# Decoder on one core: a slot table for the linear attentions, first keys and queries in the score banks, a zero block for the first bucket, the first norm's write behind the second norm's sums

## What is computed

```python
# first block: linear attention, causal by buckets of 64 tokens, 16 heads of 8 channels
q, k, v = split(x @ W_qkv.T)
q = softmax(q, axis=-1) * HEAD_DIM ** (-0.5)
k = exp(k)
# a bucket sees the sums of k and of k v over the buckets ahead of it; the first sees none
attn = q * context(shifted) / max(q . k_cumsum(shifted), 1e-06)
x = layernorm(x + attn @ W_out.T)
# second block: softmax attention a1 (16 heads of 32), then a2 on the context, each with its own
# norms and a gelu network; then a mixture of experts, a causal attention, a cross attention,
# a second mixture of experts, each with a residual and a layernorm
y = ln(x, ln1_g, ln1_b)
y = y + mha_a1(y, y);  y = ln(y, ln2_g, ln2_b);  x = layernorm(x + y + mha_a2(y, ctx))
...
```

## Time and profile before

| | |
|---|---|
| median of 3 runs | 802.41 us (798.68 to 803.11) |
| the profiled execution's own time | 800.18 us |
| its span in the profile | 798.4 us |
| busy: PE / DVE / ACT / POOL | 718.4 / 493.9 / 412.4 / 290.0 us |
| instructions | 16192 |

### The profile page before, as it was taken

The page is one execution under the profiler, slowest core; times in us unless marked ns, Lnnn a source line. Parts: engine busy times, 40 slices in busy tenths (PEclk is TensorE's granted clock), DMA queues, the critical chain, the costliest instruction groups (busy, mean ns, idle before and its releaser), DMA issues.

```text
span 798.4 us, 16192 instructions
## 1 busy us (share of the span) xinstructions
PE 718.4 (90%) x5744; PEld 532.7 (67%) x5744; DVE 493.9 (62%) x1309; ACT 412.4 (52%) x1047; POOL 290.0 (36%) x398
## 2 busy tenths in 40 slices
PE   6577899899898998999999989989898999999886
PEld 3355566675666666799898977857576455767665
DVE  3658996877968787344543456545455658684653
ACT  2124557666575676744544458655563544454311
POOL 0103564565645666310000018323431545454300
PEclk9979999999999999999999999999999656999999
DMA  7273552534627273000000000001011411000000
GB/s 242 73 187 82 122 126 68 132 70 95 136 55 204 60 202 127 1 1 1 1 1 1 1 1 4 1 1 36 6 41 50 153 63 28 5 2 9 8 7 7
DMA packets 25175, 48.10 MB, mean 60 GB/s; under 512 B 7265, under 2 KB 14193, under 8 KB 25097
## 3 DMA queue, kind: packets, MB, share of 16 engines
q1 hardware_dynamic: 24376, 45.66, 22.2%
q10 hardware_dynamic: 720, 1.41, 0.5%
HBM read 17.49 MB, written 0.52 MB: 23 GB/s over the span
## 4 chain that ended last, share of the span: by engine, by line
PE 63%; DVE 17%; issue 9%; ACT 7%; POOL 2%; DMA 1%; SPq 0%; POOLq 0%; DVEq 0%; ACTq 0%
PE G L523 8%; PE SC L778 7%; PE SC L765 7%; PE SC L708 5%; PE G L569 4%; PE SO L751 3%; DVE shift_cols L1478 3%; PE SC L800 3%; PE G L877 3%; ACT causal_probs L1092 2%; PE SC L684 2%; PE SO L832 2%; PE SM L725 2%; PE G L591 2%; PE G L528 2%
## 5 line engine op out<-in xcount | busy, mean ns | idle before, releaser
L1107 ACT ACTIVATE exps<-SC 128x512 f32<-128x512 f32 x192 | 114.1, 596 | 108.2 <-PE SC L708 107.7
L1478 DVE TENSOR_REDUCE shift_cols<-SC 128x2 f32<-128x512 f32 x192 | 129.8, 684 | 30.3 <-PE SC L684 29.5
L1557 POOL TENSOR_TENSOR rstd<-variance,consts 128x2 f32<-128x2 f32 (+1 forms) x48 | 37.2, 774 | 278.7 <-DVE variance L1171 275.6
L1626 POOL TENSOR_TENSOR VB<-exps 128x256 f32<-128x256 f32 x128 | 94.9, 749 | 63.1 <-ACT exps L1107 62.3
L1081 ACT ACTIVATE hidden<-SC,cols 128x256 f32<-128x256 f32 x128 | 53.5, 470 | 65.5 <-PE SC L765 65.3
L1648 POOL TENSOR_TENSOR causal_probs<-causal_probs,inverse 128x256 f32<-128x256 f32 x64 | 51.6, 827 | 68.9 <-DVE inverse L1491 68.9
L1512 DVE SCALAR_TENSOR_TENSOR R<-SC,small,R 128x128 f32<-128x128 f32 x128 | 39.0, 346 | 54.1 <-PE SC L778 53.5
L1092 ACT ACTIVATE causal_probs<-SC,negmax 128x128 f32<-128x128 f32 (+1 forms) x128 | 52.1, 423 | 37.2 <-DVE negmax L1486 37.0
L778 PEld LDWEIGHTS SC<-ffn_w,hidden 128*128 128x128 f32 x512 | 66.0, 192 | 5.3 <-issue 1.8
L708 PE MATMUL SC<-stacked_q,stacked_k 100*128 100x256 f32 x256 | 65.5, 338 | 3.2 <-DMA stacked_q<-shift_rows 1.6
L778 PE MATMUL SC<-ffn_w,hidden 128*128 128x128 f32 x512 | 67.6, 276 | 0.0
(11 more groups left out here) (244 smaller groups left out, 1497.7 us busy)
## 6 DMA issues: line engine op xcount, KB each, us to landing
stacked_k<-k_hi SPq DMA_DIRECT2D x64, 128.0 KB, 2.3
stacked_q<-q_hi SPq DMA_DIRECT2D x64, 128.0 KB, 2.3
ffn_w<-in_ffn_w SPq DMA_DIRECT2D x16, 512.0 KB, 4.5
stacked_k<-k_lo SPq DMA_DIRECT2D x32, 128.0 KB, 2.3
stacked_q<-q_lo SPq DMA_DIRECT2D x32, 128.0 KB, 2.3
packed_k<-U SPq DMA_DIRECT2D x48, 32.0 KB, 1.9
packed_q<-YN SPq DMA_DIRECT2D x48, 32.0 KB, 1.9
a_weights<-in_a_li SPq DMA_DIRECT2D x3, 256.0 KB, 7.8
```

The costliest lines, as they stand in the source:

```text
L1107: fn(exps[:, n % EXPS, :, :].rearrange("p t q -> p (t q)"), SC[1][:, n % 2, :, :].rearrange("p t q -> p (t q)"), ACT.Exp, scale=ATTENTIONS ...
L1478: v.tensor_reduce(shift_cols[:, n // UNIT % 4, :, n % UNIT], SC[0][:, n % 2, :, :], axis=AX.X, op=ALU.max, negate=True).then_inc(head_max, 1)
L1626: v.tensor_tensor(kept[n % EXPS].rearrange("p t q -> p (t q)"), exps[:, n % EXPS, 0, :], exps[:, n % EXPS, 1, :], ALU.add).then_inc(kept_r ...
```

## The change

Four edits, all in how the front of the program is written.

1. The slot of each step of `linear(b)` comes from a table. Batch 0 no longer shares its slots with batch 1: batch 1's first steps stand between the last ones of batch 0, and its steps from the turned queries on stand in slots -2 to 3, the last of them after the first heads. `linear(2)` begins in slot -2 and its steps up to the residual stand between slots -2 and 7.
2. The first stream's two key tiles go to the two banks of SC0 (ring "up") and its two query tiles to those of SC1 (ring "down"), which no head uses yet; the first two heads wait until these tiles have been read.
3. The first bucket, which sees no context, is multiplied by a block of zeros (`no_context`) on PE, so that numerators and denominators come as full tiles; DVE then divides them in 4 instructions in place of 6. The four zeroings of a part of Z go. The factor 8 ** -0.5 moves from a DVE instruction (L1233) into ACT's copy of the turned queries.
4. The second norm has moments and deviations of its own (indices TT on), so that X can be written after U has been measured, not ahead of U.

```diff
-def linear_at(b):
-    return (FIRST, FIRST + 1, FIRST + 9, 10)[b]
-
-
-def context_step(b):
-    return 20 if b < 2 else 9
+LINEAR_SLOTS = [
+    (-14, -14, -13, -12, -11, -10, -9, -8, -7, 6, 7, 8),
+    (-9, -8, -7, -2, -1, 0, 1, 2, 3, 8, 9, 10),
+    (-2, -2, -1, 1, 3, 5, 7, 9, 11, 13, 15, 17),
+    (10, 10, 12, 14, 16, 18, 20, 22, 24, 26, 28, 30),
+]
...
+    def due(self):
+        return self.at + self.step if isinstance(self.at, int) else self.at[self.step]
...
-    return ([Side(FIRST, linear(0))] + [Side(enter_at(b), enter(b)) for b in B]
+    return ([Side(LINEAR_SLOTS[0], linear(0))] + [Side(enter_at(b), enter(b)) for b in B]
             + [Side(project_at(s), project(s)) for s in range(2 * NB)]
-            + [Side(linear_at(b), linear(b), 1 if b == 1 else 2) for b in B[1:]]
+            + [Side(LINEAR_SLOTS[b], linear(b)) for b in B[1:]]
...
+                    pe.wait_ge(zeros_made, 1)
...
-                    for n in (1, 2, 3):
+                    for n in range(T // BUCKET):
                         r, t = BUCKET * (n % 2), n // 2
                         last = mm(g[r:r + BUCKET, t * w:(t + 1) * w], QT[b][:, n * BUCKET:(n + 1) * BUCKET],
-                                  CM[b][:, n - 1, :], start=True, stop=True)
+                                  CM[b][:, n - 1, :] if n else no_context[:, :], start=True, stop=True)
...
+                    k_ring, q_ring = ("g", "g") if s else ("up", "down")
+                    drawn(("k", s, 0), W[at["wk"]], kv, kr, 0, k_ring)
...
                     if n >= 2:
                         pe.wait_ge(head_max, n - 1)
+                    else:
+                        wait_emptied(pe, ("k", 0, n))
...
-                    copied(("qT", b), QT[b], lambda g: g[:, 0:T])
+                    copied(("qT", b), QT[b], lambda g: g[:, 0:T], HD0 ** -0.5)
...
-                    link(v.tensor_scalar(s, r, HD0 ** -0.5, None, ALU.mult))
...
+                    link(v.tensor_scalar(s.rearrange("p (t h) -> p t h", h=HEADS), num[:, :, C:C + HEADS], 1e-6, None, ALU.max))
+                    link(v.reciprocal(r, s))
+                    for t in range(TT):
+                        last = v.tensor_tensor(heads(Z[b][:, t, :]), heads(num[:, t, 0:C]),
+                                               r[:, t * HEADS:(t + 1) * HEADS].unsqueeze(2).to_broadcast([P, HEADS, HD0]),
+                                               ALU.mult)
...
-                    normalise(b, R[b], X[b])
                     link(normalise(b, R[b], U[b], k=TT))
...
-                    measure(b, U[b])
+                    measure(b, U[b], k=TT)
+                    rescaled(b, R[b], X[b], C, 0, 0)
                     if b == 0:
                         make_choice()
-                    yield 7
-                    normalise(b, U[b], Z[b]).then_inc(z_ready[b], 1)
+                    yield 8
+                    normalise(b, U[b], Z[b], mean=TT, k=TT).then_inc(z_ready[b], 1)
```

More of the change, by code:

```diff
@@ L202, with __init__ @@
 class Side:
-    def __init__(self, at, steps, pace=1):
-        self.at, self.steps, self.pace, self.step = at, steps, pace, 0
+    def __init__(self, at, steps):
+        self.at, self.steps, self.step = at, steps, 0
+    def due(self):
+        return self.at + self.step if isinstance(self.at, int) else self.at[self.step]
     def advance(self, slot):
-        while self.step is not None and self.at + self.pace * self.step <= slot:
+        while self.step is not None and self.due() <= slot:
             self.step = next(self.steps, None)
@@ L517, in enter, with drawn @@
                     yield 0
-                def drawn(key, w, src, kr, m):
-                    g = fill(pe, "g", key)
+                def drawn(key, w, src, kr, m, ring="g"):
+                    g = fill(pe, ring, key)
                     for k in range(2):
@@ L1159, in measure_part, with measured @@
                     return v.bn_stats(stats[b][:, t, :], src[:, t, 0:width])
-                def measured(b, last, again=False):
+                def measured(b, last, again=False, k=0):
                     norms[b] += 1
@@ L1166, in measured, with measure, rescaled, normalise @@
                     for t in range(TT):
-                        last = v.bn_aggr(moments[b][:, t, :], stats[b][:, t, :])
+                        last = v.bn_aggr(moments[b][:, k + t, :], stats[b][:, t, :])
                     link(last)
                     if again:
-                        v.tensor_scalar(variance[b][:, TT:2 * TT], moments[b][:, :, 1], 1 + EPS, EPS * EPS, ALU.mult, ALU.add)
-                    v.tensor_scalar(variance[b][:, 0:TT], moments[b][:, :, 1], EPS, None, ALU.add)\
+                        v.tensor_scalar(variance[b][:, TT:2 * TT], moments[b][:, 0:TT, 1], 1 + EPS, EPS * EPS, ALU.mult,
+                                        ALU.add)
+                    v.tensor_scalar(variance[b][:, k:k + TT], moments[b][:, k:k + TT, 1], EPS, None, ALU.add)\
                         .then_inc(variance_ready[b], 1)
-                def measure(b, src, width=C, again=False):
+                def measure(b, src, width=C, again=False, k=0):
                     for t in range(TT):
                         last = measure_part(b, src, t, width)
-                    measured(b, last, again)
-                def normalise(b, src, dst, width=C, k=0):
-                    dve.wait_ge(rstd_ready[b], norms[b])
+                    measured(b, last, again, k)
+                def rescaled(b, src, dst, width, mean, k):
                     for t in range(TT):
-                        last = v.tensor_scalar(dst[:, t, 0:width], src[:, t, 0:width], moments[b][:, t, 0:1],
+                        last = v.tensor_scalar(dst[:, t, 0:width], src[:, t, 0:width], moments[b][:, mean + t, 0:1],
                                                rstd[b][:, k + t:k + t + 1], ALU.subtract, ALU.mult)
                     return last
+                def normalise(b, src, dst, width=C, mean=0, k=0):
+                    dve.wait_ge(rstd_ready[b], norms[b])
+                    return rescaled(b, src, dst, width, mean, k)
                 def over_tiles(vec):
@@ L1232, in linear @@
                     link(v.reciprocal(r, s))
[L1233 to L1234 removed]
+                    v.tensor_tensor(heads(flat), heads(flat), r.unsqueeze(2).to_broadcast([P, TT * HEADS, HD0]),
                                     ALU.mult).then_inc(q_normal[b], 1)
@@ L1244, in linear @@
                         .then_inc(*emptied(("ctx", b)))
-                    yield 3
+                    yield 4
                     g = wait_filled(dve, ("num", b))
-                    dve.wait_ge(z_zeroed, b + 1)
-                    for t, r0 in ((0, BUCKET), (1, 0)):
-                        tile = g[r0:P, t * (C + HEADS):(t + 1) * (C + HEADS)]
-                        s, r = small[b][r0:P, 96:112], small[b][r0:P, 112:128]
-                        link(v.tensor_scalar(s, tile[:, C:C + HEADS], 1e-6, None, ALU.max))
-                        link(v.reciprocal(r, s))
-                        last = v.tensor_tensor(heads(Z[b][r0:P, t, :]), heads(tile[:, 0:C]),
-                                               r.unsqueeze(2).to_broadcast([P - r0, HEADS, HD0]), ALU.mult)
-                        if t == 0:
-                            link(last)
+                    num = g[:, 0:TT * (C + HEADS)].rearrange("p (t c) -> p t c", c=C + HEADS)
+                    s, r = small[b][:, 32:64], small[b][:, 64:96]
+                    link(v.tensor_scalar(s.rearrange("p (t h) -> p t h", h=HEADS), num[:, :, C:C + HEADS], 1e-6, None, ALU.max))
[4 more added lines that the diff above has]
+                                               ALU.mult)
                     last.then_inc(*emptied(("num", b)))
-                    yield 5
+                    yield 6
                     dve.wait_ge(x_in[b], 16)
@@ L1566, in _ @@
                     v.memset(V0B[b][:, :, C:C + 1], 1.0).then_inc(ones_made, 1)
-                for b in range(NB):
-                    v.memset(Z[b][0:BUCKET, 0, :], 0.0).then_inc(z_zeroed, 1)
+                v.memset(no_context[:, :], 0.0).then_inc(zeros_made, 1)
                 pool.wait_ge(consts_in, 16)
                 def linear(b):
-                    yield 5
-                    inverse_deviation(b, 2 * TT)
                     yield 6
-                    inverse_deviation(b)
-                    yield context_step(b)
+                    inverse_deviation(b, w=2 * TT)
+                    yield 7
+                    inverse_deviation(b, TT)
+                    yield 9
                     inverse_deviation(b)
```

50 lines of the change are left out of this document (27 added, 23 removed).

## The result

The changed kernel takes 807.92 us (median of 20 runs, 804.29 to 814.72); the kernel before, run beside it, takes 804.19 us (20 runs). The ratio is 1.0054, with a 95% interval of 1.0033 to 1.0075: 4 us slower, where 8 us less was predicted. The profiled execution of the changed kernel took 809.13 us.

The account below looks back on a forecast made before the run. The front was taken as bound by a latency chain, the stretch behind nearly by DVE; first head 10.7 us earlier less 3.7 us given back makes 7.0 us, so 794.3 us, range 789.5 to 799.

Parts of the forecast that it names:

- The chain to the last query tile: Front, batch 0: numerators at 11.9, Z written by 24.9, keys at 28.4, last query tile ending at 34.6 against 45.74 us.
- POOL's second deviation: Front, before Z: whether it hides behind 1.8 us of DVE work; by the port rule Z comes 0.2 us later.
- the first stack meets the weights' tail as near as before: Ahead of the first head: the weights' transfers begin 7 us earlier as well; issue to head stays 3.64 us.
- the forecast 10.7: First head at 40.6 us (bounds 39.3 and 42.5) in place of 51.28, 10.7 us earlier.
- Given back: Behind the first heads: moved DVE work of batch 1 and others, 4.6 us less 0.9 allowed for free time: 3.7 us.
- the table's other slots for batches 2 and 3 move a step by two slots at most, inside the same stretch: Behind the first heads: these steps are only shifted within the stretch; no cost was put on them.
- The one that ended slower: Rival, chance 0.04: 12 links between the heads each leave PE and DVE waiting 1.3 us, 15.6 us lost, 807 us.
- The first head hardly gains: Rival, chance 0.13: slow PE list (42.5 us), first stack behind the weights, DVE pays 5.6 us uncovered; gain 3.2, 798 us.
- No effect: Rival, chance 0.07: DVE work of streams 1 and 2 behind the front does not move and takes up all; 801 us.
- nothing is paid back: Rival, chance 0.14: DVE's free time behind the front takes the moved work; gain 9.5 to 12 us, 790.5 us.
- Theory C: From the follow-up runs' expectations: a shift in the front only moves where TensorE later falls to its lower level.
- G's wait: From the follow-up runs: ACT's split of batch 1's first key tile waits for unit 3, the first stream's fourth stack.

Follow-up runs that it names:

- keys in "g": The changed kernel with the first keys and queries back in the ring g; ratio to the kernel before 1.0042.
- unit 3 early: The changed kernel with the first stream's fourth stack issued in slot 5, ahead of the shifts of slot 6, not in slot 7; ratio to before 1.0021.
- R and G: The changed kernel with the fourth stack in slot 5 and batch 2's residual and norms in their old slots, weights left ahead of the first stack; ratio to before 0.9975.
- old slots: The changed kernel with every step of linear(b) in its slot of before, edits 2 to 4 kept; ratio to the kernel before 0.9994.
- R: The changed kernel with only the steps of linear(2) back in their slots of before; ratio to the kernel before 0.9981.
- before with unit 3 early: The kernel before with the first stream's fourth stack in slot 5 and nothing else; ratio to the kernel before 1.0009.
- weights behind the stacks: The changed kernel, weights behind the third stack: alone 1.0019, with linear(2) in old slots 0.9992; behind the fourth, issued early, batch 2's norms in old slots: 0.9893, 0.9895.
- Best: The changed kernel with the fourth stack in slot 5, the weights behind it, batch 2's residual and norms in old slots; ratio to before 0.9893, later 0.9895.

## Why the prediction was wrong

**The chain to the last query tile was right.** Numerators at 12.00 (11.9 forecast); the turning of Z0 at 26.69 (27.0), behind batch 1's bucket sums as said; keys at 28.18 (28.4); the last query tile ended at 33.61 (34.6; two tiles ran at the upper level, where one had been reckoned). The trace of the changed kernel also answers the question on POOL's second deviation:

```profile
22.23 1.17 POOL L1575 TENSOR_TENSOR rstd<-variance,consts 128x2 f32<-128x2 f32 x1 [2.64 <-DVE variance L1187]
```

It took 1.17 us beside DVE's writes, as 1.20 before, and Z was written from 23.92 us, right behind DVE's own work (24.3 forecast), so the price was nothing that shows. The Trainium skill's rule in "SBUF — State Buffer", section "SBUF: two separate sides", would have put Z 0.2 us later; its 1.17 against 0.70 alone is in keeping with the rule, its effect on the chain can't be seen here.

**The first head: the transfer was mis-sized.** The step that failed is "the first stack meets the weights' tail as near as before". Before, q_lo was issued 47.64 - 40.55 = 7.1 us behind the last weight; now only 37.02 - 33.45 = 3.6 us, in one stroke with them, and the head followed 7.7 us later. The prediction's own numbers had this: SP free of the weights at 33.8 and q_lo out at 36.8 us are 3.0 us apart, not 7.1. Over all profiles the wait follows this distance:

| profiles | end of the last weight's issue to q_lo's issue, us | q_lo's issue to the first head, us |
|---|---|---|
| changed (both), keys in "g", unit 3 early, R and G | 3.2 to 3.6 | 6.5 to 8.0 |
| old slots | 4.6 | 5.9 |
| R | 5.1 | 4.5 |
| before (both), before with unit 3 early | 5.6 to 7.1 | 2.9 to 3.6 |
| weights behind the stacks (four profiles) | none ahead | 2.5 to 3.1 |

Before the change the weights were far enough ahead to cost next to nothing. The share of the DMA engines was 1.04 while PE waited:

```profile
38.00:44.00 6.00, 0.35 (x2) 0.16 (x2) 1.38 (x5) 0.00 (x0) 0.00 (x0) 0.83 1.04 227
```

The Trainium skill says the same in "DMA: Bandwidth & Descriptors", section "Queues, rings and completion order": what one issuing engine starts is consumed on each DMA engine in the order of its ring. A copy of 128 KB then stands behind the 2.6 MB of weights issued ahead of it, and 7.7 against 3.1 us agrees. This was 4.1 us of the forecast 10.7.

**The base was one execution.** The 10.7 us were counted from 51.28 us. In the second profile the kernel before has its first head at 47.51 us and the changed one at 43.58: 3.9 us apart, not 6.6. In part the forecast took a slow front for what the kernel always does.

**Given back: twice the forecast.** Up to slot 6 the changed kernel loses 4.9 us of its lead, first against first profile: (56.75 - 44.72) less (58.44 - 51.28). That is the 4.6 us reckoned for batch 1's steps behind the first heads, with nothing absorbed: DVE is busy 9.49 of these 12.03 us, against 5.34 of 7.16 before, and PE waits 3.66 us for the maximum behind batch 1's norm. So the 0.9 us allowed for DVE's free time was wrong too. It is batch 1's row of the table: with its old slots (6.6 us from the first head to slot 6) the loss is gone, with batch 2's alone (11.6) it is not. The larger step that failed is "the table's other slots for batches 2 and 3 move a step by two slots at most, inside the same stretch". I costed it at nothing, as a count of work. But its place was what mattered: batch 2's second norm, which had stood ahead of the split of the next stream's keys, came to stand behind it, ahead of the split of the queries. From slot 6 to slot 10 the changed kernel won 4.2 us, most of it because that work was left out there (with R 2.6 of them go again); from slot 10 to slot 14 it lost 8.9, and won back 2.1 up to slot 34. That is a loss of 2.7 us behind slot 6 (second profiles: 2.9), and with the 4.9 ahead of it the 7.5 (7.8). With batch 2's old slots (R) the way from the first head to slot 34 is 111.18 - 43.00 = 68.2 us, against 72.6 in the changed kernel and 65.1 in the kernel before: 3.1 us given back, close to the 3.7 of the forecast. That closeness is partly luck, since it is 4.4 us lost up to slot 6 and 1.3 won back behind. But it is this one row of the table by which the sum failed there.

**The rivals.** The one that ended slower had the sign, and its price (807) is near; its mechanism, 1.3 us on each of twelve links, is not what happened, since a loss of 4.9 us at the first heads and waits in one place of stream 1's start made it. "The first head hardly gains" named the first stack's wait behind the weights, which was there, but took its price as up to 42.5 us. "No effect" is excluded by the interval, and "nothing is paid back" by slot 6.

**Behind slot 34** the distances between slots are those of before wherever the granted clock is the same: up to slot 66 they agree within 0.1 us in both profiles of both kernels, at 1.00. So slot 34 nearly tells the time. Changed 117.3 and 116.5: 4 us slower. R, or R and G, 111.2 and 111.4: 0.9981 and 0.9975. Best 106.2 and 106.7: 0.9893 and 0.9895. It holds to about 2 us, not closer: unit 3 early (112.89) has a ratio of 1.0021, the old slots (112.69) have 0.9994. Theory C is not the account, since the best kernel keeps in its time what it gains in slot 34, but it has a share: slots 66 to 70 take 10.9 us at 0.84 in both profiles of the changed kernel and 9.3 us at 1.00 in both of the kernel before. Single executions scatter more: from slot 34 to slot 138 the two profiles of the changed kernel take 507.5 and 516.7 us, the second with one stretch of four slots at 0.50 (15.9 us in place of 8.7). So of the 8.9 us between the spans of the two first profiles only 1.0 is there in slot 34. How much of the loss between slots 10 and 14 would go with TensorE at its upper level, and how the rest is shared between G's wait and R's, no run separates.

## What to carry to other kernels

When a table moves steps, cost the ones that "only" shift by a slot too: for each, name what it now stands ahead of on its in-order engine and who waits for that; here one row of twelve numbers cost 4.4 to 6.2 us in slot 34, and with it in its old place the changed kernel is no slower than the kernel before. Bulk loads on the queue that also carries small urgent copies belong behind those copies (or far enough ahead: 7.1 us cost next to nothing, 3.6 us cost 4), and a buffer's last reader (here a stack tied to another slot) belongs ahead of everything that waits for the buffer. Take a second profile of the kernel before: a milestone that moves by 4 us between executions can't be the base of a sum of 10.

## What the runs showed of the hardware

The same matmuls took 0.46 or 0.77 us in the front of different executions of one kernel, with the same waits around them, and the first head moved by 3.8 us with it (47.51 and 51.28); 19 of the kernel's 20 single runs lie between 798.68 and 808.24 us, more than twice the effect studied apart, and one at 817.08. A stack's last copy, 3.1 us from issue to the head with the queue free, took 7.7 us with the last weight issued 3.6 us ahead of it, and 3.6 us with 7.1 us between them. And in a wait of 2.67 us on PE the granted clock fell from 1.00 to 0.50 and stayed there for 10 us, through a second wait of 3.58 us: a query tile took 2.05 us in place of 1.10 and qkv 2.90 in place of 1.53.
